# First layer of a four-layer graph network: a row is finished in the round of its sum, one adjacency row is loaded and turned later, and the first scores wait block by block

## The chip, the core and the metric

The kernel runs on one core of a Trainium2 chip. Its engines work side by side, each through its own queue in program order, and wait for each other on semaphores: PE (TensorE, matrix products and transposes into the eight banks of PSUM), DVE (VectorE), ACT (ScalarE), POOL (GpSimd) and SP (SyncE, which here only issues DMAs). The metric is the time of one execution on the device in microseconds (us); lower is better.

## What is computed

Four layers, each followed by a residual sum and a layer norm, on x (2048 x 256) and one adjacency matrix adj (2048 x 2048, zeros and ones). The change touches only the first:

```python
def _L0_gnn_ref(x, adj, weight, bias, node_w, edge_w):
    node_att = jax.nn.softmax(x @ node_w, axis=0)
    h = x @ edge_w
    e = jnp.where(adj > 0, h @ h.T, NEG_BIG)
    edge_att = jax.nn.softmax(e, axis=1)
    return adj * (node_att * edge_att) @ (x @ weight) + bias

x = _layernorm(x + _L0_gnn_ref(x, adj, ...))
x = _layernorm(x + _L1_gnn_ref(x, adj, adj, ...))
x = _layernorm(x + _L2_gnn_ref(x, adj, ...))
x = _layernorm(x + _L3_gnn_ref(x, adj, ...))
```

## The kernel before, in words

Everything is tiled by 128: T = 16 "rows" t (128 nodes each), B = 4 blocks of 512 columns, TB = 4 rows to a block, KD = 2 feature tiles. Numbers are split into a high and a low part, so a product is three matmuls (high x high, high x low, low x high).

**Start (P0, group0).** 16 groups turn x (P0 "turn") and make h (P0 "h"), block by block; the semaphore p0_lo counts the finished low parts. Then scores(0), then 16 groups n = 16 to 31 that project one row of x each onto the support and the node weight. These use banks 4 to 7 in rotation: PE makes a group, ACT copies it (supf), DVE takes its maximum (smax), and PE may start group n when DVE has done group n - 4.

**Main part, one round for each row t.** PE: scores(t) fills banks 0 to 3 with row t of h h^T; for columns to the left it turns tiles that ACT kept of earlier rows (keep_row, tensor kept, semaphore s_kept). DVE: maxima(t) adds the mask (fill) and takes the row's maximum in two halves, which frees the banks. ACT: exp_row(t), then p_high(t), the high half of the exponents in fp16 (ph); make_fill(t + 1) makes the next mask from the adjacency row. DVE: p_low(t), the low half (pl). SP turns ph and pl by DMA into PT (turn_p, tensor turned); ph and pl are single buffers, so p_high(t + 1) waits until ph of row t has been turned, and p_low(t + 1) likewise. PE: weighted(m) sums row m against the support into bank 6 or 7; it may start when DVE has read the sum of row m - 2 (pv_read). DVE: final0(m) scales that sum and adds xb (x plus bias, added by POOL in bias_x), then takes the moments; POOL makes the reciprocal root (norm_factor); DVE: normed(m) writes the new x.

**The order.** PE runs scores(t) and behind it weighted(SUMMED[t]), with SUMMED[t] = t - 2 for t = 2 and t - 3 from t = 4 on (nothing at t = 3). DVE in round t: maxima(t), p_low(t - 1), final0 of the row that was summed on PE in round t - 1, conversions to fp16 (conv_first, only at t = 14 and 15), normed of that row. POOL: loads of adjacency rows 0 to 3, then rows 4 and 5 (row r waits for the mask of row r - 4: fill_ready), three partition reduces (the maximum of the node weights, the maximum of the support, the sum of the node exponents), rows 6 and 7, bias_x(0), bias_x(1), and then for each row: norm_factor(t), bias_x(t + 2), load of row t + 8, and at t = 5 load_later(4).

**Second loads.** Row 4 of adj and those after it are loaded a second time for the later layers (load_later into rowb) and turned by SP (turn_later). Row 4 may land in adjT only when all scores are done, since its place is used until then. Row 5 goes through the same buffer as row 4, so its load on POOL (behind the norm of row 13) waits until row 4 has been turned.

**Lines.** LATER_LOADED L108; SP's queue L417 to L455; POOL's queue L495 to L555; scores L644 to L662, weighted L664 to L678; ACT's order L1012 to L1053, with keep_row L981, make_fill L975, p_high L1003; DVE's final0 L1317, maxima L1332, round0 L1382 and the end of the layer L1424 to L1443.

## Time and profile before

| | us |
|---|---|
| median of 3 runs | 796.73 (795.49 to 796.84) |
| the profiled execution | 798.13 |
| its span in the trace | 796.3 |
| PE busy in the span | 745.1 (94%) |
| DVE busy | 450.3 (57%) |
| ACT busy | 347.1 (44%) |
| chain that ended last, PE's share | 43% |

The span is what the trace covers; 1.8 us lie around it. The first layer takes about the first 214 us of it. Busy times overlap: a matmul's record is longer than the interval at which matmuls start, so PE is busy without being at its peak. "Idle before" in brackets is how long an engine stood still ahead of an instruction, and behind the arrow stands what released it. A trailing q (SPq, POOLq) is an engine's queue rather than its datapath.

### The profile page before, as it was taken

To read this page: it belongs to the slowest core of one execution; us is meant where nothing else is said; L and a number is where in the kernel's file an instruction comes from. 1 tells how busy PE (TensorE), PEld (TensorE's weight loads), DVE (VectorE), ACT (ScalarE), POOL (GpSimd) and SP (SyncE) were. 2 spreads that over 40 slices of the span, in tenths; PEclk is the share of its full clock that TensorE was granted. 3 is DMA by queue.
4 is the path that set the end of the run, shared out by engine and by line. 5 is a ranking of instruction groups with operands and counts; after the bars stand their busy time and mean duration, and the time that the engine had idled before them with its cause. 6 is when DMAs were issued, how large, how long until landed. Compare 5 with 4: busy or idle time off the path is not lost.

```text
span 796.3 us, 11711 instructions
## 1 busy us (share of the span) xinstructions
PE 745.1 (94%) x4213; PEld 493.5 (62%) x4256; DVE 450.3 (57%) x934; ACT 347.1 (44%) x530; POOL 105.9 (13%) x214
## 2 busy tenths in 40 slices
PE   6888999797999999999979989999999999999997
PEld 5776766464678877787735644665664546465443
DVE  4476888688768787979843475120262311114465
ACT  4668876675385474746521233231361322224000
POOL 1011222111321020101011130000001000000343
PEclk9999999999999999999999999999999999999999
DMA  8947998996549509100030000000000000000011
GB/s 225 188 84 133 167 175 151 170 154 118 99 87 164 75 2 185 41 1 1 1 86 1 0 1 0 1 0 0 0 0 27 1 1 0 0 0 1 20 40 47
DMA packets 114300, 48.71 MB, mean 61 GB/s; under 512 B 103504, under 2 KB 109776, under 8 KB 114256
## 3 DMA queue, kind: packets, MB, share of 16 engines
q1 hardware_dynamic: 110224, 33.44, 21.6%
q0 software_dynamic: 4032, 14.68, 10.7%
q8 instruction: 27, 0.44, 0.2%
q14 instruction: 17, 0.14, 0.1%
HBM read 35.53 MB, written 2.10 MB: 47 GB/s over the span
## 4 chain that ended last, share of the span: by engine, by line
PE 43%; DVE 7%; issue 2%; ACT 2%; POOL 0%; POOLq 0%; ACTq 0%; DVEq 0%
PE ps L756 11%; PE ps L911 10%; PE ps L889 8%; PE ps L946 4%; PE ps L920 3%; PE ps L872 3%; PE ps L936 2%; PE ps L612 1%; DVE x L1553 1%; DVE stats L1275 1%; DVE es_lo L1263 1%; DVE tm L1473 1%; DVE agg_lo L1461 0%; PE ps L764 0%; DVE y L1675 0%
## 5 line engine op out<-in xcount | busy, mean ns | idle before, releaser
L756 PE MATMUL ps<-adjT,x 128*128 (+1 forms) x737 | 169.3, 380 | 8.9 <-DVE x L1553 4.3
L756 PEld LDWEIGHTS ps<-adjT,x 128*128 128x128 f16 x768 | 71.7, 98 | 90.2 <-issue 6.0
L675 PE MATMUL ps<-sup,turned 128*128 128x512 f16 x256 | 88.4, 394 | 12.2 <-DVE y L1328 12.2
L1263 DVE TENSOR_TENSOR hh_lo<-hf,hh_hi 128x512 fp32r<-128x512 f32 x32 | 22.1, 692 | 134.6 <-ACT hf L1199 133.5
L911 PE MATMUL ps<-adjT,G 128*128 x375 | 82.6, 379 | 0.9 <-ACT hf L1199 0.4
L806 PE MATMUL ps<-H_hi,es_hi 128*128 128x258 f32 x256 | 76.6, 299 | 2.2 <-DVE es_lo L1263 1.7
L806 PE MATMUL ps<-H_hi,es_lo 128*128 128x258 f32 x256 | 72.5, 283 | 0.0
L806 PE MATMUL ps<-H_lo,es_hi 128*128 128x258 f32 x256 | 72.4, 283 | 0.0
L677 PE MATMUL ps<-sup,turned 128*128 128x256 f16 x256 | 71.8, 280 | 0.0
L911 PEld LDWEIGHTS ps<-adjT,G 128*128 128x128 f16 x384 | 37.2, 98 | 45.4 <-issue 0.9
L1089 ACT ACTIVATE es_hi<-tm 128x1024 fp32r<-128x1024 f32 x32 | 33.9, 1058 | 55.3 <-DVE tm L1473 55.2
L491 POOL TENSOR_TENSOR rstd<-mv,epsc 128x1 f32<-128x1 f32 x64 | 14.8, 232 | 315.4 <-DVE mv L1277 315.4
L675 PEld LDWEIGHTS ps<-sup,turned 128*128 128x128 f16 x256 | 25.8, 101 | 46.8 <-DVE y L1328 14.7
L806 PEld LDWEIGHTS ps<-H_hi,es_hi 128*128 128x128 f32 x256 | 48.4, 189 | 7.3 <-DVE es_lo L1263 4.5
L806 PEld LDWEIGHTS ps<-H_lo,es_hi 128*128 128x128 f32 x256 | 48.5, 190 | 0.4
L806 PEld LDWEIGHTS ps<-H_hi,es_lo 128*128 128x128 f32 x256 | 48.4, 189 | 0.0
L1263 DVE TENSOR_TENSOR es_lo<-tm,es_hi 128x1024 fp32r<-128x1024 f32 x32 | 39.2, 1225 | 14.8 <-issue 6.8
L1461 DVE SCALAR_TENSOR_TENSOR agg_lo<-ps,agg_hi 128x512 fp32r<-128x512 f32 x24 | 16.1, 687 | 55.0 <-ACT agg_hi L1082 55.0
L1473 DVE SCALAR_TENSOR_TENSOR tm<-slrow,ex,nb 128x512 f32<-128x512 f32 x64 | 45.3, 749 | 1.1
L1306 DVE CUSTOM_DVE_ANT_0 em<-ps,fill 128x1024 f32<-128x1024 f32 x32 | 38.0, 1216 | 13.1 <-ACT kept L989 7.4
L1197 ACT ACTIVATE hh_hi<-ps,b2c,g 128x512 fp32r<-128x512 f32 x16 | 12.5, 778 | 72.2 <-PE ps L911 48.1
L946 PE MATMUL ps<-x,adjT 128*128 128x512 f16 x192 | 41.8, 379 | 1.9 <-DVE y L1675 1.9
(216 smaller groups left out, 1478.3 us busy)
## 6 DMA issues: line engine op xcount, KB each, us to landing
adjb<-in_adj POOLq DMA_DIRECT2D x16, 512.0 KB, 6.8
adjf<-in_adj POOLq DMA_DIRECT2D x12, 512.0 KB, 5.9
x<-in_x SPq DMA_DIRECT2D x4, 512.0 KB, 7.2
out<-adjf SPq DMA_DIRECT2D x16, 128.0 KB, 1.7
adjf<-in_L_gnn_W SPq DMA_DIRECT2D x1, 1024.0 KB, 5.8
W1f<-in_L_gnn_W SPq DMA_DIRECT2D x1, 512.0 KB, 3.7
adjf<-in_L_gnn_W SPq DMA_DIRECT2D x1, 512.0 KB, 3.8
we<-in_L_gnn_edge_w SPq DMA_DIRECT2D x1, 256.0 KB, 3.9
```

The source lines that it names most:

```text
L675: ins = mm(bank(6 + u), PT(HI, t)[:, jt, :], sup[:, jt, :], start=(jt == 0), stop=False, skip_group_check=True)
L677: ins = mm(bank(6 + u, D), PT(LO, t)[:, jt, :], sup[:, jt, 0:D], start=False, stop=(jt == T - 1), skip_group_check=True)
L756: ins = mm(bank(4 + f), x16[:, part, jt, f * P:(f + 1) * P], adj(b, jt), start=(jt == 0 and part == HI), stop=(jt == T - 1 and part == LO))
L806: ins = mm(bank(k, D + 2), es[p][:, (b * T + jt) % RE, k * P:(k + 1) * P], H[q][:, jt, :], start=(jt == 0 and (p, q) == (HI, HI)), stop=(j ...
L872: ins = mm(bank(o % 2), W1s[p][:, k, o * P:(o + 1) * P], agg[q][:, k, :], start=(k == 0 and (p, q) == (HI, HI)), stop=(k == KD - 1 and p = ...
L889: ins = mm(bank(to, width), hh[p][:, o, k * P:(k + 1) * P], ws[q][:, o, :], start=(o == 0 and (p, q) == (HI, HI)), stop=(o == KH - 1 and p ...
L911: ins = mm(bank(4 + o), g16(jt, part, o * P, P), adj(b, jt), start=(jt == 0 and part == HI), stop=(jt == T - 1 and part == LO))
L946: ins = mm(bank(u), adjT[:, bass.ds(b, 1), jt, k * P:(k + 1) * P].rearrange("p a c -> p (a c)"), f16[:, jt, :], start=(jt == 0), stop=(jt ...
L1089: own.link(run(es[HI][:, s, :], tm[:, s, :], ACT.Exp, scale=SLOPE - 1.0))
L1263: return tt(to, frm, high.bitcast(F32), ALU.subtract)
L1306: nc.vector.tensor_tensor_reduce(out=em[:, u, cols], in0=banks, in1=fill[:, t % 2, cols], scale=1.0, scalar=-3.0e38, op0=ALU.add, op1=ALU.max,
L1473: stt(tm[:, (b * T + jt) % RE, :], slrow[:, b * CB:(b + 1) * CB], ex[:, jt, 0:1], nb[:, jt % 2, :], ALU.add, ALU.max).then_inc(tm_ready, 1)
```

## The change

- SP: the turning of row 4 no longer stands between rows 14 and 15 of the exponents, but behind all of them.
- POOL: row 4 is loaded the second time behind row 9's norm factor, not row 5's.
- PE: scores(0) waits for each block of h ahead of the bank that needs it, not once for all.
- ACT, start: one more projection copy ahead of p_high(0); make_fill(1) behind the last projection copy. ACT, main part: keep_row(3) moves from behind p_high(2) to ahead of it.
- DVE: in round t normed of the row summed in the round before comes right behind maxima(t), and final0 of the row that PE sums in this same round ends the round. At the end of the layer, two of the conversions move behind final0 of row 12.

```diff
--- before.py
+++ after.py
@@ -105,7 +105,7 @@
 
     TURNS, GROUP, KEPT = T // 2, 4 * KD * P, 3
 
-    LATER_LOADED = {5: 4}
+    LATER_LOADED = {9: 4}
 
 
 
@@ -436,11 +436,9 @@
             for t in range(T):
                 turn_p(t, HI)
                 turn_p(t, LO)
-                if t == T - 2:
-                    sp.wait_ge(e_mm, B * T)
-                    turn_later(TB)
-
-            for t in (TB + 1,):
+
+            sp.wait_ge(e_mm, B * T)
+            for t in (TB, TB + 1):
                 turn_later(t)
             sp.wait_ge(xb_ready, T)
             sp.dma_start(brow[:, :], vec_row(bg_in)).then_inc(bias1_landed, 16)
@@ -643,13 +641,13 @@
 
             def scores(t):
 
-                if t == 0:
-                    pe.wait_ge(p0_lo, P0_SUP)
                 own = t - (t % TB == TB - 1) if t >= TB else 0
                 wait_from(pe, s_kept, banks_kept(t, -1))
                 if t == TB:
                     pe.wait_ge(row0_placed, 1)
                 for c in range(B):
+                    if t == 0:
+                        pe.wait_ge(p0_lo, P0.index(("h", c, KD - 1)) + 1)
                     if c % 2 == 0:
                         wait_from(pe, e_read, 2 * (t - 1) + c // 2 + 1)
                     for m in range(TB * c, min(own, TB * c + TB)):
@@ -1017,12 +1015,12 @@
             for n in range(P0_SUP, P0_SUP + 2):
                 group0(n)
             exp_row(0)
-            for n in range(P0_SUP + 2, P0_SUP + 6):
+            for n in range(P0_SUP + 2, P0_SUP + 7):
                 group0(n)
             p_high(0)
+            for n in range(P0_SUP + 7, P0_GROUPS):
+                group0(n)
             make_fill(1)
-            for n in range(P0_SUP + 6, P0_GROUPS):
-                group0(n)
             place_row0()
             act.wait_ge(node_neg, 1)
             run(nl[:, :], nl[:, :], ACT.Exp, bias=nst[:, 2:3], accum_out=nst[:, 3:4]).then_inc(node_exp, 1)
@@ -1044,11 +1042,13 @@
             keep_row(2)
             p_high(1)
             for t in range(2, T):
-                if t > 2:
+                if t > TB - 1:
                     keep_row(t)
                 if t + 1 < T:
                     make_fill(t + 1)
                 exp_row(t)
+                if t + 1 == TB - 1:
+                    keep_row(t + 1)
                 p_high(t)
                 conv_high(HIGH_ROUND.get(t, ()))
             conv_high(range(10, 13))
@@ -1381,15 +1381,15 @@
 
             def round0(t):
 
-                u = t % 2
-                maxima(t, u)
-                p_low(t - 1, 1 - u)
-                m = SUMMED.get(t - 1)
-                if m is not None:
-                    final0(m, m % 2)
+
+                maxima(t, t % 2)
+                if t - 1 in SUMMED:
+                    m = SUMMED[t - 1]
+                    normed(m, m % 2, x[:, m, :])
+                p_low(t - 1, (t - 1) % 2)
                 conv_first(LOW_ROUND.get(t, ()))
-                if m is not None:
-                    normed(m, m % 2, x[:, m, :])
+                if t in SUMMED and t < T - 1:
+                    final0(SUMMED[t], SUMMED[t] % 2)
 
             maxima(0, 0)
             for t in range(T):
@@ -1422,9 +1422,8 @@
                 if t == 7:
                     weight_parts()
             p_low(T - 1, 1)
-            conv_first(range(9, 11))
             final0(T - 4, 0)
-            conv_first(range(11, 12))
+            conv_first(range(9, 12))
             normed(T - 4, 0, x[:, T - 4, :])
             final0(T - 3, 1)
             conv_first(range(12, 13))
```

## Rows read from the trace of the kernel before

**Rows 1.** Stretches: window, length, busy PE, PEld, DVE, ACT, POOL, clock, DMA.

```profile
80.00:143.90 63.90, 63.01 (x382) 44.19 (x381) 55.25 (x114) 50.18 (x61) 12.67 (x25) 1.00 0.94 164
143.90:183.60 39.70, 33.50 (x205) 22.47 (x205) 30.50 (x61) 27.56 (x35) 6.83 (x14) 0.91 0.88 148
156.90:165.80 8.90, 8.87 (x42) 5.08 (x43) 7.60 (x15) 5.76 (x7) 1.99 (x4) 0.70 0.98 174
```

**Rows 2.** Timeline of PE: start, us, engine, line, operation, then idle before.

```profile
25.68 0.50 PE L661 MATMUL ps<-hT_hi 128*128 128x512 f32 x1 [1.41 <-DVE hT_lo L1263]
...
73.89 0.44 PE L656 MATMUL ps<-ident,kept 128*128 128x128 f32 x1 [3.44 <-DVE mx L1306]
...
79.94 0.39 PE L675 MATMUL ps<-sup,turned 128*128 128x512 f16 x1
...
156.93 0.61 PE L675 MATMUL ps<-sup,turned 128*128 128x512 f16 x1 [4.91 <-DVE y L1328]
...
183.62 0.39 PE L675 MATMUL ps<-sup,turned 128*128 128x512 f16 x1 [1.26 <-DVE y L1328]
...
192.85 0.47 PE L675 MATMUL ps<-sup,turned 128*128 128x512 f16 x1 [3.86 <-DVE y L1328]
...
202.06 0.39 PE L675 MATMUL ps<-sup,turned 128*128 128x512 f16 x1 [1.27 <-DVE y L1328]
```

**Rows 3.** Timeline of DVE, from the maximum of row 10 to that of row 11.

```profile
137.45 1.21 DVE L1306 CUSTOM_DVE_ANT_0 em<-ps,fill 128x1024 f32<-128x1024 f32 x1
...
145.62 0.81 DVE L1268 TENSOR_SCALAR x<-y,mv,rstd 128x256 f32<-128x256 f32 x1 [0.94 <-POOL rstd L492]
146.35 1.21 DVE L1306 CUSTOM_DVE_ANT_0 em<-ps,fill 128x1024 f32<-128x1024 f32 x1
```

**Rows 4.** Lines L515, L499, L577: count, ns min/median/max, first and last start.

```profile
L515 POOLq MODIFY_POOL_CONFIG  x2: 37/37/37, 41.8 to 41.8; - x2
...
L499 POOLq MODIFY_POOL_CONFIG  x4: 42/62/83, 68.3 to 729.4; - x4
...
L577 POOLq MODIFY_POOL_CONFIG  x2: 11/11/11, 484.2 to 484.2; - x2
```

**Rows 5.** Timeline of POOL.

```profile
49.80 0.64 POOL L515 PARTITION_ALL_REDUCE nst<-nst  x1 [8.01 <-DVE nst L1401]
...
77.85 1.84 POOL L499 TENSOR_TENSOR xb<-x,brow 128x256 f32<-128x256 f32 x2 [9.61 <-issue]
...
137.92 0.54 POOL L534 DMA_DIRECT2D adjf<-in_adj  x1
...
490.12 0.38 POOL L577 PARTITION_ALL_REDUCE wm<-wm  x1 [12.53 <-issue]
```

**Rows 6.** Timeline of DVE: maximum of the node weights, first reading of row 0's sum.

```profile
48.78 0.16 DVE L1401 TENSOR_REDUCE nst<-nl 128x1 f32<-128x16 f32 x1
...
79.15 0.48 DVE L1326 SCALAR_TENSOR_TENSOR y<-ps,rowf,xb 128x256 f32<-128x256 f32 x1
```

**Rows 7.** Timeline of ACT: fills of rows 1 and 3.

```profile
38.71 1.92 ACT L979 ACTIVATE fill<-adjb 128x2048 bf16<-128x2048 bf16 x1
...
65.16 1.91 ACT L979 ACTIVATE fill<-adjb 128x2048 bf16<-128x2048 bf16 x1
```

**Rows 8.** Timeline of SP's queue: low half of row 9, second turning of row 4.

```profile
142.35 5.50 SPq L432 DMA_TRANSPOSE turned<-pl x1
...
193.67 3.32 SPq L425 DMA_TRANSPOSE adjT<-adjf  x1
```

**Rows 9.** Timeline of DVE: end of row 15's maximum, then its low half.

```profile
188.76 0.21 DVE L1340 TENSOR_SCALAR negm<-mx 128x1 f32<-128x1 f32 x1
...
197.43 2.36 DVE L1315 SCALAR_TENSOR_TENSOR pl<-em,ph 128x1024 f16<-128x1024 f32 x2 [1.34 <-DMA turned<-pl]
```

**Rows 10.** DMA issues of 10 to 240 us: count, median us from issue to landing.

```profile
turned<-ph SPq DMA_TRANSPOSE x16, 6.3
turned<-pl SPq DMA_TRANSPOSE x16, 4.4
```

## The prediction

> **What bounds the kernel now.** I read the page first, then the stretches, then the engines' timelines inside the first layer. The change touches only the first layer, which fills the first 214 us, so the chain of waits of the later layers matters only for one thing: whatever the first layer gives or takes is handed on in full, because its last weighted sum releases everything after it. I call S(t) the scores of row t on PE, W(m) the weighted sum of row m on PE, and round t what DVE does from the maximum of row t on.
>
> In the stretches [rows 1] the reader is to see two regimes. From 80 to 144 us PE is busy 63.0 of 63.9 us: PE is the bound there, and only 0.9 us can be had. From 144 to 184 us it is busy 33.5 of 39.7 us, and part of that is work at the lower clock (mean 0.91). PE's own timeline [rows 2] says where it stands idle: 1.4 us ahead of the first scores, 3.4 ahead of S(4), 4.9 ahead of W(9), 1.3, 3.9 and 1.3 ahead of W(12), W(13) and W(14), each time until DVE has read or written something. A round of DVE [rows 3] takes 8.90 us (137.45 to 146.35); 0.94 of it is waiting for POOL's reciprocal root ahead of the norm, and the norm takes 0.81.
>
> **The change, part by part.** I carry one shift (after minus before) through the layer.
>
> *First scores.* S(0) no longer waits for all of h. Its first bank needs only block 0, and the last bank comes 4.2 us later, when block 3 is there. PE goes on directly: 24.1 instead of 25.68 [rows 2], shift -1.6. ACT's copies of row 0 were waiting for PE and follow.
>
> *Projection, then the fill of row 1.* ACT now does five projection copies instead of four ahead of the high half of row 0, then the rest, and the fill only after the last. The fifth copy waits for PE (which waits for a DVE maximum) until about 36.2, the high half ends at 38.5, and copy, maximum and PE's next group need 1.1 us more: PE resumes at 39.6 and does five groups of 0.72 us, to 43.3. At the lower clock for about half of that, as in the run of before, it would be some 1.7 later (an estimate); PE's idle time here is shorter, so I take the higher clock. The last copy ends at 43.8, the fill of row 1 (2.0 us and its accumulator) at 45.9 instead of 40.7 [rows 7]: shift **+5.1** of the fill, although PE itself is 4 us ahead.
>
> *What hangs on that fill.* POOL's queue holds, in this order: the load of row 5, which waits for the fill of row 1; then the first partition reduce. Ahead of that reduce stands a MODIFY_POOL_CONFIG, issued at 41.8 [rows 4]. The reduce began at 49.80 [rows 5] although its input, DVE's 0.16 us reduction at 48.78 [rows 6], had been ready for 0.9 us. So this configuration took 8.0 us. Nothing else in the trace explains the gap; where nothing is loading it took 5.9 (484.2 to 490.12) [rows 4, 5]. Today it is hidden behind the projection. After, it starts 5.1 later, at 47.0, and I give it 8.3, because a transpose now also falls into it (bounds 5.9 and 9.5): the first reduce starts at 55.3, +5.5. Behind it in the queues wait DVE's scale and maximum of row 1, and ACT's exponent of the node weights with the keeping of row 1 behind it. Of the 5.5, ACT takes over 4.2: before, DVE passed the reduce's result on 0.8 later than it was there (it was in the low half of row 0), and ACT's third copy of row 1 waited 0.5 for PE, which is now long done. The early gain of PE is thereby gone. Then the scaled support, the fill of row 2, the exponent of row 1 and the fill of row 3 follow on ACT without a gap: fill of row 3 at +4.2 [rows 7].
>
> *A row's sum in its own round.* The sum of row 0 is finished in DVE's round 2 instead of 3, so ahead of the maximum of row 3. It needs xb of row 0, POOL's first addition after the reduces. That has a second configuration ahead of it (68.3 [rows 4]), behind the load of row 7, which waits for the fill of row 3; the addition began at 77.85 [rows 5], 9.5 us later, and ended at 79.0. In the run of before DVE reaches it at 79.15 [rows 6], just in time, one round later. After, POOL is at +4.2: xb is there at 83.2, while DVE has nothing left from about 72. So **DVE stands still for some 11 us ahead of the maximum of row 3**: sum and moments take 1.8 more, and the maximum starts at 85.2. The early copying of row 3 (keep_row(3) ahead of the high half of row 2) would have brought that maximum 2.5 us forward; this wait swallows it. S(4) waits for its first half and starts at 86.5 instead of 73.89 [rows 2], +12.6. PE has by then been idle for some 9 us instead of 3.4, and I add 0.5 to S(4) for a longer time at the lower clock. W(1) begins at 93.0 instead of 79.94: shift **+13.1**. Bounds: both configurations at 5.9 give +7; both at 9.5, with the lower clock in the projection, +16.
>
> The Trainium skill bears on this place: "GPSIMD Engine Reference", section 2.1, says that the first call of a freshly loaded kernel pays about 6 us that no instruction shows (5.95 measured) and should be budgeted for. The trace agrees with a figure of that size where no DMA is under way (5.9) and has 8.0 and 9.5 where one is. With 5.95 at both places the sum below would end 5.9 us lower, at 790.3.
>
> *Rounds 4 to 15.* DVE's round loses the wait of 0.94 and, since POOL no longer adds beside the norm, up to 0.4 of its 0.81: 7.6 us. The new wait is for W(m) of the same round, and the next row's maximum is queued behind it, with ACT's exponent after that. Behind S(t) DVE needs half a maximum (1.2 and 0.2), the norm 0.4, the low half 2.3 and three small steps 0.6, together 4.7; W takes 5.2 (an estimate from the busy time of a round at full clock). So PE is the bound as long as DVE's round has nothing extra. From W(1) to W(8) that gives back only the idle part of the first stretch: -0.9.
> From W(8) to W(12) PE's work is the 33.5 busy us [rows 1] less 2.6 for W(9) at the lower clock (8.9 us at a mean of 0.70 [rows 1]), which it no longer meets without the idle time ahead: 30.9 instead of 39.7 us, **-8.8**. This is the largest gain, and its main part is the load of row 4: it is issued at 137.92 [rows 5], right behind another load, the transpose behind them sits 5.5 us in SP's queue [rows 8], and PE idles 4.9. After, it is issued in the round of row 9's sum (round 12), by when no other load is left: the loads move a round earlier with the sums. I cost its one transfer beside transposes at nothing, since rows are two rounds ahead there; without that cover 2 us. W(12) starts at 93.0 + 63.1 + 30.9 = 187.0 instead of 183.62 [rows 2], shift +3.4.
>
> *The end of the layer.* DVE was late: the maximum of row 15 ended at 188.9 [rows 9], 5.3 behind the start of W(12). Now it is early, save for 1.4 us of conversions in round 14 that W doesn't wholly cover: 3.3 behind, at 190.3. W(13) now follows W(12) at once. But W(14) needs the sum of row 12, which still stands behind the low half of row 15, and that behind the landing of the low half of row 14. Before, DVE could start on row 15 only at 197.43 [rows 9], 6.2 us behind that issue, with the transposition of row 4 (193.67 [rows 8]) in the same stretch. After: 4.6 us, as in other rounds (median of all low halves 4.4 [rows 10]). From the end of the last maximum to W(14): 0.3 + 2.3 + 0.1 + 4.6 + 2.3 + 0.6 + 1.0 = 11.2 instead of 13.2 us. W(14) at 201.6 instead of 202.06: shift **-0.5**. The conversions of rows 9 and 10 now stand behind the sum, beside W(14). The transposition of row 4 comes last; POOL waits for it ahead of loading row 5, lands about 206, and POOL gets there at about 207; if it is late, POOL's roots of rows 14 and 15 are late with it (0 to 1 us).
>
> **Sum:** +13.1 (W(1)) - 0.9 - 8.8 = +3.4 (W(12)); 5.3 becomes 3.3, -2.0; 13.2 becomes 11.2, -2.0; rounded -0.5 for W(14) and all behind it. The profiled execution took 798.13 for a span of 796.3; span 795.8 gives 797.6 for it. The median of the three runs is 796.73, so **796.2**.
>
> **Rivals.**
> *A (forecast), 0.60:* both configurations bite; own range 793.5 to 799.
> *B, 0.15: the standstill isn't there, or is short.* The two gaps of POOL could be waits that I misread, or overlap more. For it: the engine's rows show only "issue". Against: the same gap behind each such instruction. Without the +13 the shift would be down to -13; half of it is likelier, 783 to 791.
> *C, 0.25, slower: the single buffer of the high half takes PE's place as bound.* The copy of row t+1 on ACT waits until row t has been turned. Median landing is 6.3 us [rows 10], with 2.0 of copying and 0.3 of issue 8.7 us a round. Now DVE's 8.9 hides it. It decides as soon as a round would be shorter than 8.7: from W(7) on. Seven rounds from W(5) to W(12) at 8.9 make 62.3 instead of 56.8: +5.5, so 801.7; if only those rounds with loads suffer, 798.5. Against: with 4.5 where no load is in the way a round needs 6.8.
> That parts of the change don't do what they say: the early copy of row 3 is one such (price nothing, as worked above).
>
> **Chances.** 0.2% is 1.6 us, about what a measurement of this kernel can tell from no change. Faster (under 795.1): 0.20 of A and all of B, 0.35. Same: 0.30 of A and 0.04 of C, 0.34. Slower (over 798.3): 0.10 of A and 0.21 of C, 0.31. Range 787 to 801: it leaves out the better half of B and the worst fifth of C.
>
> **What would show it.** First PE scores at 24.1; first partition reduce near 55; xb near 82 and DVE idle for about 11 us ahead of the sum of row 0; S(4) from 86; W(1) at 93; rounds of 8.6, then 7.6 us with DVE waiting for PE and not for POOL; no idle ahead of W(9); W(14) near 201.6. A partition reduce near 50, or a maximum of row 3 before 75, makes this wrong on the fast side; PE waits ahead of W(8) to W(12) on the slow side.

## The result, and the profile after

| | before | after |
|---|---|---|
| median, us | 796.28 (795.49 to 796.84, 4 runs) | 804.01 (802.98 to 805.46, 4 runs) |
| profiled execution, us | 798.13 | 803.83 |
| its span, us | 796.3 | 802.0 |

The ratio is 1.0077, 95% interval 1.0053 to 1.0102: slower by 0.8%. The forecast was 796.2 with a range of 787 to 801, so the time lies outside it, on the slow side. Here and below the medians count every execution, while the ratios leave out those more than 1.5% above the fastest of the same kernel.

The timeline of PE after, with the starts that answer to [rows 2] (start, us, engine, line, operation, idle before and its releaser): the first scores, S(2), S(4), then W(1), W(8), W(9), W(12), W(13), W(14), W(15).

```profile
23.32 0.39 PE L659 MATMUL ps<-hT_hi 128*128 128x512 f32 x1
...
57.60 0.76 PE L659 MATMUL ps<-hT_hi 128*128 128x512 f32 x1 [9.59 <-DVE mx L1306]
...
85.50 0.45 PE L654 MATMUL ps<-ident,kept 128*128 128x128 f32 x1 [9.00 <-DVE mx L1306]
...
92.27 0.39 PE L673 MATMUL ps<-sup,turned 128*128 128x512 f16 x1
...
154.91 0.39 PE L673 MATMUL ps<-sup,turned 128*128 128x512 f16 x1
...
162.83 0.39 PE L673 MATMUL ps<-sup,turned 128*128 128x512 f16 x1
...
186.24 0.39 PE L673 MATMUL ps<-sup,turned 128*128 128x512 f16 x1
...
192.13 0.38 PE L673 MATMUL ps<-sup,turned 128*128 128x512 f16 x1 [0.52 <-DMA turned<-pl]
...
205.64 0.61 PE L673 MATMUL ps<-sup,turned 128*128 128x512 f16 x1 [7.25 <-DVE y L1328]
...
214.13 0.38 PE L673 MATMUL ps<-sup,turned 128*128 128x512 f16 x1
```

W(1) is 12.3 us later than before (79.94), W(12) only 2.6 (183.62); the 4.9 us idle ahead of W(9) are gone. But W(14) is 3.6 later (202.06) and W(15), which began at 208.61 before, 5.5. From W(15) to the end both spans have 587.7 to 587.9 us, so the whole loss is there at W(15), and more than half of it arises behind W(12) (2.9 of 5.5 us).

Four stretches of the same trace (window, length, busy PE, PEld, DVE, ACT, POOL, granted clock, DMA share, GB/s): W(1) to W(8), W(8) to W(12), W(12) to W(14), W(14) to W(15).

```profile
92.27:154.91 62.64, 62.64 (x382) 44.28 (x382) 55.88 (x121) 48.20 (x57) 13.15 (x27) 1.00 0.97 167
154.91:186.24 31.33, 30.98 (x207) 21.57 (x206) 24.97 (x52) 24.57 (x32) 5.99 (x12) 1.00 0.99 165
186.24:205.64 19.40, 11.63 (x83) 7.09 (x81) 15.37 (x34) 8.94 (x14) 1.44 (x3) 0.93 0.61 113
205.64:214.13 8.49, 8.49 (x44) 4.96 (x45) 6.95 (x22) 2.24 (x3) 4.63 (x8) 0.76 0.60 114
```

In the first two PE is never idle for more than 0.35 us in all. In the third it works 11.6 of 19.4 us, and in the fourth it works all the time, at a mean clock of 0.76: the first of W(14)'s matmuls takes 0.61 us, those of the other sums shown 0.38 or 0.39.

The front, on POOL and DVE: the load of row 5, the first reduce, xb of row 0 and its first reader, the maximum of row 3.

```profile
45.39 0.53 POOL L505 DMA_DIRECT2D adjb<-in_adj  x1 [15.14 <-ACT fill L977]
54.42 0.38 POOL L513 PARTITION_ALL_REDUCE nst<-nst  x1 [8.50 <-issue]
...
81.36 1.40 POOL L497 TENSOR_TENSOR xb<-x,brow 128x256 f32<-128x256 f32 x2 [10.07 <-issue]
...
82.23 0.48 DVE L1326 SCALAR_TENSOR_TENSOR y<-ps,rowf,xb 128x256 f32<-128x256 f32 x1 [11.09 <-POOL xb L497]
...
84.12 1.23 DVE L1306 CUSTOM_DVE_ANT_0 em<-ps,fill 128x1024 f32<-128x1024 f32 x1
```

And the end of the layer: ACT's high half of row 13 and what follows it, then DVE from the second half of row 14's maximum to the sum of row 12.

```profile
179.95 2.01 ACT L1009 ACTIVATE ph<-em 128x1024 f16<-128x1024 f32 x2 [2.26 <-DMA turned<-ph]
181.86 1.32 ACT L1038 ACTIVATE x<-x 128x256 f16<-128x256 f32 x4
183.09 0.26 ACT L987 ACTIVATE kept<-ps 128x128 f32<-128x128 f32 x1
...
183.51 1.23 DVE L1306 CUSTOM_DVE_ANT_0 em<-ps,fill 128x1024 f32<-128x1024 f32 x1 [1.13 <-issue]
...
187.50 1.43 DVE L1370 SCALAR_TENSOR_TENSOR x<-x 128x256 f16<-128x256 f32 x4
...
191.37 1.23 DVE L1306 CUSTOM_DVE_ANT_0 em<-ps,fill 128x1024 f32<-128x1024 f32 x1
...
193.78 0.21 DVE L1340 TENSOR_SCALAR negm<-mx 128x1 f32<-128x1 f32 x1
...
201.66 2.36 DVE L1315 SCALAR_TENSOR_TENSOR pl<-em,ph 128x1024 f16<-128x1024 f32 x2 [3.40 <-DMA turned<-pl]
...
204.58 0.48 DVE L1326 SCALAR_TENSOR_TENSOR y<-ps,rowf,xb 128x256 f32<-128x256 f32 x1
```

The second half of row 14's maximum waits 1.13 us. The profile names no releaser; in the program it may start only when ACT has kept row 14 (183.09 to 183.35). On ACT this keeping stands behind four conversions, which stand behind the high half of row 13, and that waited 2.3 us for its buffer. The maximum of row 15 ends at 193.99, 7.75 us behind the start of W(12), and in the kernel before it ended 5.3 behind it [rows 2, 9].

### The profile page after: what moved, and what is told of

Same layout as the page of the kernel before. It is cut to its first block, busy times and chain, and to the rows that moved or that the text cites. A ratio compares the mean times of both kernels' runs of the same rounds, so it can differ in the third digit from the quotient of the medians.

```text
span 802.0 us, 11754 instructions
## 1 busy us (share of the span) xinstructions
PE 747.2 (93%) x4256; PEld 494.0 (62%) x4256; DVE 446.7 (56%) x934; ACT 347.5 (43%) x530; POOL 104.4 (13%) x214
## 4 chain that ended last, share of the span: by engine, by line
PE 43%; DVE 7%; issue 2%; ACT 2%; POOL 0%; POOLq 0%; ACTq 0%; DVEq 0%
PE ps L754 11%; PE ps L909 10%; PE ps L887 8%; PE ps L944 4%; PE ps L918 3%; PE ps L870 3%; PE ps L934 2%; PE ps L610 1%; DVE x L1552 1%; DVE stats L1275 1%; DVE es_lo L1263 1%; DVE tm L1472 1%; DVE agg_lo L1460 0%; PE ps L762 0%; DVE y L1672 0%
## 5 line engine op out<-in xcount | busy, mean ns | idle before, releaser
L754 PE MATMUL ps<-adjT,x 128*128 128x512 bf16 (+1 forms) x768 | 174.6, 379 | 6.7 <-DVE x L1552 3.9
L673 PE MATMUL ps<-sup,turned 128*128 128x512 f16 x256 | 86.1, 386 | 7.8 <-DVE y L1328 7.3
L1089 ACT ACTIVATE es_hi<-tm 128x1024 fp32r<-128x1024 f32 x32 | 33.9, 1059 | 55.4 <-DVE tm L1472 55.3
```

The lines of the kernel that those rows point to most:

```text
L673: ins = mm(bank(6 + u), PT(HI, t)[:, jt, :], sup[:, jt, :], start=(jt == 0), stop=False, skip_group_check=True)
L754: ins = mm(bank(4 + f), x16[:, part, jt, f * P:(f + 1) * P], adj(b, jt), start=(jt == 0 and part == HI), stop=(jt == T - 1 and part == LO))
L1089: own.link(run(es[HI][:, s, :], tm[:, s, :], ACT.Exp, scale=SLOPE - 1.0))
```

## The experiments

Sixteen kernels, each timed beside the kernel before on the same chip. The difference is the ratio less one times 797 us.

| kernel | median, us | ratio and interval | difference |
|---|---|---|---|
| after | 804.01 | 1.0077 (1.0053 to 1.0102) | +6.1 |
| e5: before, fill of row 1 late | 803.88 | 1.0087 (1.0070 to 1.0104) | +6.9 |
| e9: after, small load of row 4 | 803.68 | 1.0083 (1.0063 to 1.0103) | +6.6 |
| e15: after, conversions late | 803.46 | 1.0065 (1.0047 to 1.0083) | +5.2 |
| e10: after, sum 12 early | 801.89 | 1.0055 (1.0036 to 1.0075) | +4.4 |
| e2: after, row 0's sum in round 3 | 801.35 | 1.0054 (1.0035 to 1.0073) | +4.3 |
| e19: e9 and e15 together | 801.34 | 1.0043 (1.0028 to 1.0058) | +3.4 |
| e3: after, bias_x early | 800.69 | 1.0042 (1.0023 to 1.0061) | +3.3 |
| e14: e7 with both POOL moves | 799.01 | 1.0022 (1.0005 to 1.0038) | +1.8 |
| e1: after, fill of row 1 as before | 798.72 | 1.0013 (0.9998 to 1.0029) | +1.0 |
| e4: after, both POOL moves | 798.28 | 1.0019 (0.9989 to 1.0050) | +1.5 |
| e7: before, row 4 later | 794.48 | 0.9967 (0.9948 to 0.9986) | -2.6 |
| e11: e1 and e10 together | 793.73 | 0.9947 (0.9926 to 0.9967) | -4.2 |
| e16: e7, sum 12 early | 792.98 | 0.9950 (0.9924 to 0.9977) | -4.0 |
| e18: e13, sum 12 early | 792.93 | 0.9926 (0.9899 to 0.9953) | -5.9 |
| e13: e1 with DVE's order of before | 792.40 | 0.9936 (0.9914 to 0.9958) | -5.1 |
| e20: e11, row 0's sum in round 3 | 788.90 | 0.9877 (0.9857 to 0.9898) | -9.8 |

### The ledger: which part costs what (e1, e5, e7, e13)

e1 is the kernel after with ACT's start order of before; e5 the kernel before with ACT's start order of after.

```diff
+            for n in range(P0_SUP + 2, P0_SUP + 6):
-            for n in range(P0_SUP + 2, P0_SUP + 7):
                 group0(n)
             p_high(0)
+            make_fill(1)
-            for n in range(P0_SUP + 7, P0_GROUPS):
+            for n in range(P0_SUP + 6, P0_GROUPS):
                 group0(n)
-            make_fill(1)
```

> The changed kernel with ACT's order at the start as before (four projection copies, high half of row 0, fill of row 1, then the other copies). Theory 1 (the loss comes from two configurations in POOL's queue, each ahead of work that DVE waits for): the first partition reduce, at 54.4 us in the changed kernel, starts near 49, xb of row 0 near 79, W(1) near 89 instead of 92.3, and the whole is 2 to 4 us shorter than the changed kernel, 800 to 802. Rival 2 (the loss is that DVE now waits for PE's sum of the same round; the start only seems to matter): W(1) may move, but the time stays within 1 us of 804, since the rounds behind it would stretch to what PE and DVE need together.

> The kernel before with ACT's new order at the start alone (five projection copies, the fill of row 1 behind the last). Theory 1: the load of row 5, and with it POOL's first configuration, goes 4 to 5 us later, the first reduce to 54 instead of 49.80, W(1) to 83 to 84 instead of 79.94. How much of this reaches the end tells how much slack the rounds have: 3 to 4 us if none, 800 to 801; under 1 us if the turning of the halves by DMA sets the pace of the rounds anyway.

The fill's place costs 5.1 us in the one kernel and 6.9 in the other, each more than its theory 1 had (e1 at 800 to 802, e5 at 800 to 801). In e5 the load of row 5 goes out at 48.55 and the first reduce follows 8.51 us of "issue" later; in e1 they are back early, and everything behind is earlier by the same: first reduce 48.12 (6.3 earlier than after), W(1) 85.05 (7.2), W(12) 178.40 (7.8). No round gives any of it back. (This execution of e1, 796.10, lies 2.6 us below the kernel's median, so what its trace shows is larger than the 5.1 us of the ratios.) The timelines of POOL, first in e5, then in e1:

```profile
48.55 0.53 POOL L507 DMA_DIRECT2D adjb<-in_adj  x1 [18.76 <-ACT fill L979]
57.59 0.38 POOL L515 PARTITION_ALL_REDUCE nst<-nst  x1 [8.51 <-issue]
```

```profile
48.12 0.38 POOL L513 PARTITION_ALL_REDUCE nst<-nst  x1 [8.68 <-issue]
```

e7 is the kernel before with only row 4's part of the change. e13 is e1 with DVE's order of before too, so it keeps of the change row 4's part, the first scores by blocks and keep_row(3) early.

```diff
 e7, against before
-    LATER_LOADED = {5: 4}
+    LATER_LOADED = {9: 4}
...
-                if t == T - 2:
-                    sp.wait_ge(e_mm, B * T)
-                    turn_later(TB)
...
-            for t in (TB + 1,):
+            sp.wait_ge(e_mm, B * T)
+            for t in (TB, TB + 1):
                 turn_later(t)
 e13, against e1
+                if t == 3:
+                    dve.wait_ge(p_lo, 4)
                 maxima(t, t % 2)
-                if t - 1 in SUMMED:
-                    m = SUMMED[t - 1]
-                    normed(m, m % 2, x[:, m, :])
                 p_low(t - 1, (t - 1) % 2)
+                m = SUMMED.get(t - 1)
+                if m is not None:
+                    final0(m, m % 2)
                 conv_first(LOW_ROUND.get(t, ()))
-                if t in SUMMED and t < T - 1:
-                    final0(SUMMED[t], SUMMED[t] % 2)
+                if m is not None:
+                    normed(m, m % 2, x[:, m, :])
...
             p_low(T - 1, 1)
+            conv_first(range(9, 11))
             final0(T - 4, 0)
-            conv_first(range(9, 12))
+            conv_first(range(11, 12))
```

> The kernel before with row 4's second load in row 9's place on POOL and its turning behind all others, nothing else. Theory 1: the 4.9 us of idle PE ahead of W(9) and its lower clock go, 5 to 7 us at W(12); at the end of the layer the turning is out of the way of the low half of row 14, 1 to 2 us more: 789 to 793. Rival 3 (DMA is one serial resource that paces the rounds, the load only moves its collision): a wait for the turned high half appears two rounds later and at most 2 us are won, 794 to 797.

> The changed kernel with two parts undone: ACT's start order (fill of row 1 behind four projection copies) and DVE's order (the sum of a row finished one round later, its norm at the end of that round). What is left of the change: the first scores' waits by blocks, row 4's second load and turn, keep_row(3) early. Compared with the changed kernel less ACT's start order alone (798.7). Theory 1, DVE's new order costs time by itself (it makes DVE stand still ahead of the maximum of row 3 until xb is there, 10.4 us with ACT's order undone, and the last sum before the end of the layer stands behind the low half of row 15): maximum of row 3 about 8 us earlier, 793.5 to 794.5. Theory 2, the order is neutral because the rounds of rows 4 to 12 absorb what they are given: 798 to 799.

Put one behind the other, the four steps lead from before to after: row 4's part -2.6 (e7), first scores and keep_row(3) together -2.5 (e7 to e13), DVE's order +6.1 (e13 to e1), the fill +5.1 (e1 to after); sum +6.1. Each ratio is known to about 0.2%, so a step, being a difference of two, is known to some 2 us; and the shares depend on the order in which the parts are taken, as the two prices of the fill show. e13 is 1 us faster still than theory 1 had it. Two parts gain, two lose more.

In e7 the idle time ahead of W(9) is 0.83 instead of 4.91 us, as theory 1 had it, but the time, 794.5, lies where rival 3 put it: ACT waits for the turned high half two rounds later (1.51 us at row 11, 2.58 at row 12), and PE stands idle 1.05 and 1.63 us ahead of W(10) and W(11).

```profile
151.73 0.39 PE L673 MATMUL ps<-sup,turned 128*128 128x512 f16 x1 [0.83 <-DVE y L1326]
...
161.47 2.00 ACT L1009 ACTIVATE ph<-em 128x1024 f16<-128x1024 f32 x2 [2.58 <-DMA turned<-ph]
```

W(8) to W(12) takes 39.7 us before, 35.9 in e7 and 36.7 in e13, but 30.7 in e1. So row 4's part gives less than half of the gain of that stretch; DVE's order gives the rest.

DVE's order is not simply bad. In e13 W(2) starts at 86.47 and W(12) at 177.60, 9.11 us a round; in e1 it is 94.62 to 178.40, 8.38 a round. The new order loses 8.2 us up to W(2) and wins 7.3 of them back (xb of row 0 is there at the same time in both, 74.15 and 74.31). What it loses for good comes behind W(12): W(14) starts 18.3 us behind W(12) in e13 and 19.4 in e1, and W(15) 6.6 behind that in e13 and 8.7 in e1. At W(15) e1 is 4.1 us behind e13 in these two executions, where the ratios say 6.1. The timelines of PE, W(14) in e13, then in e1:

```profile
195.87 0.39 PE L673 MATMUL ps<-sup,turned 128*128 128x512 f16 x1 [1.57 <-DVE y L1328]
```

```profile
197.76 0.61 PE L673 MATMUL ps<-sup,turned 128*128 128x512 f16 x1 [7.21 <-DVE y L1328]
```

### Is DVE's standstill a price? (e2, e20, e3, e4, e14)

e2 and e20 finish row 0's sum one round later, as before; e2 does it on the kernel after (its edit is shown), e20 on e11. The added wait, which e13 and e18 have too, is met already by DVE's own order and only makes it explicit.

```diff
+                if t == 3:
+                    dve.wait_ge(p_lo, 4)
                 maxima(t, t % 2)
-                if t - 1 in SUMMED:
-                    m = SUMMED[t - 1]
+                due = {**{r: SUMMED[r] for r in range(4, T)}, 3: 0}
+                if t - 1 in due:
+                    m = due[t - 1]
...
-                if t in SUMMED and t < T - 1:
-                    final0(SUMMED[t], SUMMED[t] % 2)
+                if t in due and t < T - 1:
+                    final0(due[t], due[t] % 2)
```

e3 puts bias_x(0) and bias_x(1) ahead of the loads of rows 6 and 7 on the kernel after; e4 also puts the load of row 5 behind the reduces. e14 is both of these on e7.

> The changed kernel, but the sum of row 0 is finished in DVE's round 3 (as before the change), all later rows in their own round. Theory 1: DVE no longer stands still for 11 us ahead of the maximum of row 3; the standing still goes behind that maximum and S(4) runs beside it, so W(1) comes 8 to 9 us earlier, near 84, and the time falls by 6 to 9 us against the changed kernel, to 795 to 798. Rival 2: the rounds from 4 on are unchanged and hold the loss, so at most 2 us are won.

> The changed kernel, but POOL adds xb of rows 0 and 1 ahead of the loads of rows 6 and 7, right behind the third partition reduce. The same instructions, only the second configuration now starts near 56 instead of 71 us. Theory 1: xb of row 0 is there by 66, DVE doesn't wait for it, S(4) starts 10 to 11 us earlier (near 75) and the time is 8 to 12 us below the changed kernel, 792 to 796. Rival 2: at most 2 us are won. Rival 3 (the end of the layer gives everything back, because the rounds are bound by the turning of the high half): W(1) 11 us earlier, but less than half of it at the end.

> As the run with the early additions, and the load of row 5 also goes behind the reduces, so that the first configuration starts near 30 us, behind the load of row 4, and is over long before the node maximum is there. Theory 1: the first reduce starts near 44 instead of 54.4, the maximum of row 1 near 46 instead of 56.2, and another 8 to 10 us are won at W(1) against the run with the early additions alone; of that 5 to 10 reach the end: 783 to 789. Rival 3: W(1) moves, the end by less than 3 us.

> The kernel before with row 4's second load behind row 9's norm factor and its turning last, plus POOL's first steps moved: the load of row 5 behind the three reduces, bias_x(0) and bias_x(1) ahead of the loads of rows 6 and 7. Compared with the same without POOL's moves (794.5). Theory 1, the front of the layer sets the end: first reduce from 50.3 to about 44.5, W(1) from 77.3 to about 72, 789 to 791. Theory 2, the rounds behind are paced by the turning of the high half on a single buffer beside the loads, which are now denser (rounds of 9.9 us against 8.5 in the changed kernel with the same moves): gain at the front given back, W(12) within 1.5 us of where it was, 793.5 to 795.

> The changed kernel with ACT's start order of before, the sum of row 12 finished ahead of the conversions and low half of row 15, and row 0's sum finished in round 3 of DVE, behind the low half of row 2, as before. Compared with the same without the last edit (793.7). Theory 1, the standstill ahead of the maximum of row 3 is a price by itself, since the rounds behind it are bound by PE at 8.4 us: W(1) from 85 to about 74, W(2) to about 86.5, all of it kept, 785.5 to 788. Theory 2, the rounds of rows 5 to 10 are then paced by the adjacency loads and the turned high half, which no edit at DVE brings forward (rounds over 9 us and waits of 3 to 5 us on ACT for the turned high half): at most 2 us kept, 791.5 to 793.7.

e2 takes away DVE's standstill of 11 us and keeps 1.8 of it, as its rival 2 had it. e3 brings W(1) to 81.33, 10.9 us earlier, and keeps 2.8, less than half, as its rival 3 had it. e4 brings the first reduce to 44.80, xb to 55.61 and W(1) to 72.42, 20 us earlier, and keeps 4.6. Against the kernel after, 8.1 of these 20 us are gone already between W(1) and W(2) (17.7 us instead of 9.6), none from W(2) to W(8) (53.1 us in both), and 6.6 from W(8) to W(12) (37.9 instead of 31.3). In the first and the last of these stretches the chain is the same: ACT waits for the turned high half, its keeping of a row comes late, and DVE's maximum or PE's scores wait for that. First the high halves of rows 2 and 3 on ACT, DVE's maximum of row 4 and PE behind it; then the high half of row 13 and the scores behind it:

```profile
70.61 2.00 ACT L1009 ACTIVATE ph<-em 128x1024 f16<-128x1024 f32 x2 [3.80 <-DMA turned<-ph]
...
79.01 2.00 ACT L1009 ACTIVATE ph<-em 128x1024 f16<-128x1024 f32 x2 [2.52 <-DMA turned<-ph]
...
81.67 1.23 DVE L1306 CUSTOM_DVE_ANT_0 em<-ps,fill 128x1024 f32<-128x1024 f32 x1 [7.00 <-ACT kept L987]
...
83.05 1.30 PE L654 MATMUL ps<-ident,kept 128*128 128x128 f32 x5 [5.27 <-DVE mx L1306]
...
173.75 2.00 ACT L1009 ACTIVATE ph<-em 128x1024 f16<-128x1024 f32 x2 [4.47 <-DMA turned<-ph]
```

Between 70 and 174 us ACT has nine such waits in e4, of 1.1 to 4.5 us. Not each costs something: 3.97 us at 117.48 lie in the stretch that takes as long as in the kernel after. In e14 POOL's moves even cost 4.4 us, which neither theory allowed for. Its POOL issues the loads of rows 5 and 6 back to back (x2), SP's transposes behind them are slow, ACT waits for the turned high half, and the keeping of row 3, which in this order stands behind that high half, holds DVE for 10 us:

```profile
59.47 1.29 POOL L505 DMA_DIRECT2D adjb<-in_adj  x2
...
63.21 4.50 SPq L432 DMA_TRANSPOSE turned<-ph  x1
67.76 4.58 SPq L432 DMA_TRANSPOSE turned<-pl  x1
...
72.75 2.00 ACT L1009 ACTIVATE ph<-em 128x1024 f16<-128x1024 f32 x2 [5.69 <-DMA turned<-ph]
...
75.53 1.22 DVE L1304 CUSTOM_DVE_ANT_0 em<-ps,fill 128x1024 f32<-128x1024 f32 x1 [9.98 <-ACT kept L987]
```

So the single buffer of the high half does hold up some rounds once the front is earlier (rival C's mechanism). In the kernel after ACT waits for it too, up to 3.5 us, but from W(1) to W(12) PE stands still for 0.35 us in all. With the fill back and the last sum early, e20 keeps 5.6 us of the 11 by the ratios (-4.2 to -9.8), and 4.8 by the medians: neither theory's range (785.5 to 788, 791.5 to 793.7) holds 788.9. Five of its six executions lie at 787.0 to 789.9; the profiled one took 798.63, and its trace shows what that execution meets. These are three of ACT's waits for the turned high half; beside them PE stands still for 5.65, 3.24 and 2.81 us:

```profile
147.26 2.00 ACT L1009 ACTIVATE ph<-em 128x1024 f16<-128x1024 f32 x2 [8.44 <-DMA turned<-ph]
...
159.52 2.00 ACT L1009 ACTIVATE ph<-em 128x1024 f16<-128x1024 f32 x2 [5.90 <-DMA turned<-ph]
...
178.99 2.00 ACT L1009 ACTIVATE ph<-em 128x1024 f16<-128x1024 f32 x2 [3.85 <-DMA turned<-ph]
```

e20 is the fastest version here, 1.2% below the kernel before, but one execution in six met such landings.

### The end of the layer (e9, e15, e19, e10, e11, e16, e18)

```diff
 e9: row 4's second load moves 256 of 2048 columns
-                nc.gpsimd.dma_start(rowb[k], adj_in[t * P:(t + 1) * P, :])...
+                cols = N // 8 if t == TB else N
+                if t == TB:
+                    own.link(nc.gpsimd.memset(rowb[k][:, cols:N], 0.0))
+                nc.gpsimd.dma_start(rowb[k][:, 0:cols], adj_in[t * P:(t + 1) * P, 0:cols])...
 e15: conversions out of ACT's round 13 and DVE's round 14
-    HIGH_ROUND = {T - 4: range(0, 2), T - 3: range(2, 6), T - 2: range(6, 10)}
-    LOW_ROUND = {T - 2: range(0, 4), T - 1: range(4, 9)}
+    HIGH_ROUND = {T - 4: range(0, 2), T - 2: range(2, 10)}
+    LOW_ROUND = {T - 1: range(0, 9)}
 e10: the sum of row 12 ahead of the last conversions and low half
-                conv_first(LOW_ROUND.get(t, ()))
-                if t in SUMMED and t < T - 1:
+                if t < T - 1:
+                    conv_first(LOW_ROUND.get(t, ()))
+                if t in SUMMED:
                     final0(SUMMED[t], SUMMED[t] % 2)
...
+            conv_first(LOW_ROUND[T - 1])
             p_low(T - 1, 1)
-            final0(T - 4, 0)
             conv_first(range(9, 12))
```

e19 is e9 and e15 together (in both e9 and e19 the adjacency of row 4 is incomplete in the later layers, and POOL's clearing stands ahead of the load, which goes out at 176.73 in e9 instead of 174.37). e11 has e10's edit on e1; e16 and e18 have the same move in the order of before, on e7 and on e13.

> The changed kernel, but the second load of row 4 moves only its first 256 of 2048 columns; POOL clears the rest (the adjacency of this row is left out there). In the changed kernel the high half of row 12 takes 8.0 us from issue to landing beside this load (5 otherwise), ACT waits 2.3 us for it, keeps row 14 late, and the maximum of row 14 is late. Theory 3 (the collision costs what the prediction had at nothing): that landing is under 6 us, the maximum of row 15 ends 2.5 to 3.5 us earlier against the start of W(12), and the whole is 2 to 4 us below the changed kernel, 800 to 802. Rival (the late point is ACT's four conversions, not the load): less than 1 us.

> The changed kernel with the conversions of rows 0 to 9 to fp16 taken out of round 13 of ACT and round 14 of DVE: ACT does them behind the high half of row 14, DVE ahead of the low half of row 15. Theory 1, the maximum of row 15 is late (7.75 us behind the start of W(12), forecast 3.3) because these steps stand ahead of it: 1.3 us on ACT ahead of the keeping for row 14 and 1.4 on DVE: maximum 2 to 2.7 earlier, W(14) as much earlier, 801.5 to 802. Theory 2, the round of row 14 is bound by PE and the landing of the high half of row 12 (2.3 us of waiting on ACT): maximum at most 1.4 earlier and the low half of row 15 later by DVE's longer conversions, 803 to 804.5.

> The changed kernel with both suspects of the last rounds removed at once: row 4's second load moves only 256 of its 2048 columns (the rest is set to zero, so the adjacency of row 4 is incomplete in the later layers), and the conversions of rows 0 to 9 are out of round 13 of ACT and round 14 of DVE. Alone, the first gave 803.7 and the second 803.5 against 804.0. Theory 1, the two stood side by side and each covered the other (without the conversions ACT waited 4.7 us for the turned high half of row 12, without the load DVE and ACT still had 1.4 and 1.3 us of conversions): now the second half of the maximum of row 14 starts near 182.3, the maximum of row 15 ends near 191, 4.7 us behind W(12), and W(14) starts near 203: 800.5 to 801.8. Theory 2, the round of row 14 is that long by the new order alone: maximum of row 15 still 6.5 us or more behind W(12), 803 to 804.

> The changed kernel with the rule for a row's sum carried through: the sum of row 12 is finished in round 15, ahead of the five conversions and of the low half of row 15, which waits for the low half of row 14 to be turned. In the changed kernel W(14) waits 7.25 us for that sum and then runs at the lower clock. Theory 4 (the end of the layer is a chain low half of row 14, landing, low half of row 15, sum of row 12, W(14)): W(14) then waits only for the turned row 14 and starts near 202 instead of 205.6, W(15) 4 to 5 us earlier, the time 3 to 5 us below the changed kernel, 799 to 801. Rival: W(15) is held by the turned row 15 anyway, under 1 us.

> The changed kernel with ACT's start order of before, and with the sum of row 12 finished on DVE ahead of the conversions and the low half of row 15. With the first edit alone 798.7; the second alone took 2.1 us from the changed kernel. Theory 1, the two prices lie at opposite ends of the layer and add: 796.4 to 797. Theory 2, the end of the layer is held by the turned low half of row 14 whatever the sum's place: 798 to 798.7.

> The kernel before with row 4's second load behind row 9's norm factor and its turning last, and in addition the sum of row 12 finished on DVE right behind the norm of row 11, ahead of the conversions of rows 4 to 8 and of the low half of row 15. Compared with the same without the last edit (794.5), where PE stood idle 1.7 us ahead of W(14). Theory 1, that idle time is the wait for the sum of row 12 behind the low half of row 15: gone, the end of the layer 1.2 to 2 us earlier, 792.5 to 793.3. Theory 2, W(14) is then held by the turned low half of row 14, or the low half of row 15 comes later by as much and W(15) pays: 794.2 to 795.

> The fastest so far (first scores by blocks, row 4 later, keep_row(3) early; ACT's start order and DVE's order of before: 792.4) and in addition the sum of row 12 finished ahead of the conversions and the low half of row 15. Theory 1, the idle 1.6 us ahead of W(14) go: 790.8 to 791.4. Theory 2, W(15) is held by the low half of row 15, which is later by as much: 792 to 793.

Neither suspect alone changes the time clearly: 803.7 without the load, 803.5 without the conversions. Their traces say why. In e9 ACT waits 0.36 instead of 2.26 us for the turned high half, and the maximum of row 15 starts at 190.62 instead of 191.37, since the conversions still stand there. What is left of that at W(14) (204.86 instead of 205.64) is lost in W(14) itself, at a mean clock of 0.69: W(15) starts at 214.30, after at 214.13. In e15 the conversions are gone, and the wait takes their place:

```profile
182.31 2.00 ACT L1009 ACTIVATE ph<-em 128x1024 f16<-128x1024 f32 x2 [4.72 <-DMA turned<-ph]
184.22 0.26 ACT L987 ACTIVATE kept<-ps 128x128 f32<-128x128 f32 x1
...
191.16 1.23 DVE L1306 CUSTOM_DVE_ANT_0 em<-ps,fill 128x1024 f32<-128x1024 f32 x1
```

Together (e19) they give 2.7 us, as theory 1 had it by the time, but the interval of e19 (to 1.0058) still touches that of the kernel after (from 1.0053). The trace kept of e19 is of an execution of 815.78 us, so the new times of its steps are not shown. That the two cover each other is what the times suggest.

The last sum's place is worth 2.1 us by the medians in the kernel after (e10, where theory 4 had 3 to 5) and 5.0 with the fill back (e11, where theory 1 had about 2). The timelines of PE, W(14) in e10, then in e11:

```profile
204.55 0.38 PE L673 MATMUL ps<-sup,turned 128*128 128x512 f16 x1 [3.36 <-DMA turned<-pl]
```

```profile
194.26 0.38 PE L673 MATMUL ps<-sup,turned 128*128 128x512 f16 x1 [3.38 <-DMA turned<-pl]
```

W(14) then waits for the turned low half of row 14 and no longer for DVE: 15.5 us behind W(12) in both. The traces agree on what the move gives behind W(12): from there to W(15) it is 23.7 us in e10 and 23.8 in e11, and 27.9 and 28.1 without it, so 4.2 and 4.3 us. But in e10's profiled execution W(12) itself started 2.8 us later than in that of after, ahead of anything the edit touches: PE waits 0.87 and 1.92 us for rows that ACT kept late. Whether e10's other executions met this too is not shown. And the clock falls in W(14) of e10 and e11 as well, some matmuls in: it runs at a mean of 0.79 behind 3.4 us of idle time, and W(14) to W(15) takes 8.21 us in both, instead of 6.55 in e13, where PE had stood idle 1.57 us. In the order of before the same move is worth 1.5 us by the medians on e7 (e16, with overlapping intervals) and nothing on e13 (e18, as its theory 2 had it).

e18 and e20 differ only in DVE's order from round 4 on: both have the fill in its old place, row 0's sum in round 3 and the last sum early. e20, with the new order, is 3.9 us faster by the ratios, and the intervals are apart. So the new order, +6.1 us in the ledger, gains once its first round and its last are mended.

## Why the prediction was wrong, step by step

- **First scores: right.** 23.32 instead of 25.68 (forecast 24.1). Of that 1.1 us are not the change: the first product of h starts at 9.10 instead of 10.19, since x landed earlier in this execution.
- **Fill of row 1 and the first configuration: right, and this was one of the two losses (5.1 to 6.9 us).** Fill at 42.85, 4.1 later (forecast 5.1: the projection ended 1 us earlier than I had it, and the whole started 1.1 us earlier). The configuration took 8.5 of idle "issue" instead of 8.3, first reduce at 54.42 (forecast 55.3). e1 and e5 confirm it from both sides.
- **A figure of the Trainium skill.** By the Trainium skill's page "GPSIMD Engine Reference", section 2.1, both gaps would have been 5.95 us. Here they were 8.5 and 10.1 us with DMAs under way: the measurement decides against it, and the forecast was right to take the longer ones.
- **The standstill: right in place and size, wrong in price.** DVE waited 11.09 us for xb (forecast 11), S(4) 85.50 (86.5), W(1) 92.27 (93.0). But e2 shows that taking it away gives back 1.8 us in this kernel, and e20 about 5 in e11, not 11. Rival B put 6 to 13 us on its absence, more than either.
- **Rounds 4 to 12: right in size, wrong in its main part.** W(1) to W(8) -1.3 and W(8) to W(12) -8.4 us against -0.9 and -8.8 (62.6 and 31.3 us instead of 63.9 and 39.7), no idle time ahead of W(9), W(12) at 186.24 instead of 187.0. But I had called the load of row 4 the main part of the 8.8; e7, with row 4's part alone, wins 3.7 us there, and e1 against e13 gives DVE's order 6.0.
- **The maximum of row 15: the step that failed.** "3.3 behind, at 190.3": it ended at 193.99, 7.75 behind. Of the 3.3 I had given 1.4 to conversions, which leaves 1.9. In the kernel after, the maximum of row t ends 2.3 to 3.8 us behind the start of W(t - 3) for rows 4 to 11, but 4.8 for row 12, 5.0 for row 13, 7.0 for row 14 and 7.75 for row 15: DVE falls behind over four rounds. By my own count it needs 7.6 us for a round, and PE's rounds here are down to 7.5 (170.53 to 177.99 for W(10) to W(11)), so it has no reserve to catch up with. What makes it late is in part rival C's mechanism, to which the forecast itself had given no price: the high halves of rows 10, 11 and 13 wait 2.52, 3.53 and 2.26 us on ACT for the turned one, the keeping behind each is late, and the second halves of the maxima of rows 11, 12 and 14 stand 1.14, 1.57 and 1.13 us. The wait of row 11's high half, and the maximum of row 12 behind it:

```profile
163.58 2.01 ACT L1009 ACTIVATE ph<-em 128x1024 f16<-128x1024 f32 x2 [3.53 <-DMA turned<-ph]
...
166.13 1.23 DVE L1306 CUSTOM_DVE_ANT_0 em<-ps,fill 128x1024 f32<-128x1024 f32 x1 [1.57 <-issue]
```

Conversions of 1.43 us and 0.47 for the turned low half came on top. How the 4.45 us divide among these is not shown. Row 4's load, costed at nothing in round 12, was worth 0.75 us at that maximum (e9; 1.7 counted from W(1), which started 0.9 later there).

- **From that maximum to W(14): right.** 11.65 instead of 11.2.
- **W(14) itself: the second step that failed, a term put at nothing.** PE had stood idle 7.25 us and runs it at a mean clock of 0.76: W(14) to W(15) 8.49 us instead of 6.55 before, +1.9.
- **The sum.** -0.8 (W(12)) + 4.45 + 0.45 + 1.9 = +6.0, of the 6.2 us between the forecast span (795.8) and the measured one (802.0).

The outcome that I gave 0.31, slower, came about, but not where I had it: rival C had PE waiting ahead of W(8) to W(12), and PE did not wait there. Its buffer did delay DVE there, which is likely part of the idle time ahead of W(14).

## What to carry to other kernels

Moving work within one engine's queue moves everything that its semaphore releases: one mask, put behind the last ten copies, delayed a load, the load delayed a configuration on POOL, and 5 to 7 us went through to the end. A new order that shortens the steady round must be costed at both of its ends too: its first round, where a tile it needs earlier isn't there, and its last, where nothing follows that could absorb a late step. When two suspects stand side by side, take both away at once before you acquit either. And look at where a gain is lost stretch by stretch: an average round hides that e4 loses nothing of its 20 us in six rounds and 15 in five others.

## What the runs showed that I had not expected

- **The configuration on POOL has no fixed length.** The first one took 7.8 to 9.6 us in fourteen traces, 8.7 in e1 among them, but in e13, with the same front as e1, the first reduce came 5.87 us behind the load of row 5 and was released by DVE's input and not by "issue" (45.71 against 48.12); e18 has 7.30 in the same way. The second took 9.4 to 10.4 us where adjacency loads stand ahead of it, and 6.6 to 7.6 where bias_x comes first (e3, e4, e14). It starts at its place in POOL's queue, not when its first user's input is ready: with nothing gating it (e4, e14) all of the first one is hidden.
- **An earlier front can make the layer slower.** e14, whose first reduce starts 3.3 us earlier than e7's and whose last 1.5, is 4.4 us slower. In its trace the transposes behind two loads issued back to back take 4.5 us each, and DVE stands still for 10 us behind them; that these loads are the cause was not tested by itself.
- **One kernel, two lengths.** Five of e20's executions lie at 787.0 to 789.9 and one at 798.6; in that one ACT waited up to 8.4 us for the turned high half. e3 has five at 800.3 to 801.7 and one at 806.0, where ACT waited up to 8.1 us. I don't know what starts such an execution.
